# First local attention of a hybrid network: values as narrow weights on four column strips, probabilities weighed by GpSimd, output head-major in one bank

## The chip, the cores and the metric

The kernel runs on one core of one Trainium2 chip. The time is device time in microseconds of one execution, from the start of the program to its end. A core has TensorE (matmuls; its clock is granted at one of two levels, 1.2 or 2.4 GHz, and the profile shows the share), VectorE, ScalarE and GpSimd (elementwise work), and SyncE, which issues DMAs. In the profile they are PE (with its weight loads as PEld), DVE, ACT, POOL and SP. They run unsynchronised, each through its own program in order, and wait for each other on semaphores. TensorE writes to PSUM, eight banks of 128 partitions by 512 fp32; GpSimd doesn't read PSUM in this kernel.

## What is computed

A network of eight blocks in a row on x of 4 sequences ("lanes") by 512 tokens by 128 features, each block a layer norm, a sub-network and a residual. The change touches the first sub-network alone: four layers of attention and MLP. Of its 8 heads, each 16 wide, four are local (a window of 128 tokens looks at itself and at the window before it, causally), four are causal linear attention over buckets of 64 tokens:

```python
def local_attn(q, k, v):                       # heads 0 to 3, WINDOW 128
    bq, bk, bv = ...                           # windows of 128 tokens
    bk2, bv2 = look_around(bk), look_around(bv)  # window before, own window
    dots = jnp.einsum('bwie,bwje->bwij', bq, bk2) * e ** (-0.5)
    dots = jnp.where(causal_mask | pad_mask, mask_value, dots)
    attn = jax.nn.softmax(dots, axis=-1)
    return jnp.einsum('bwij,bwje->bwie', attn, bv2)

def causal_linear_attn(q, k, v):               # heads 4 to 7, BUCKET 64
    q, k = softmax(q), elu(k) + 1.0
    ctx = cumsum(einsum('bhund,bhune->bhude', bk, bv)) / (cumsum(k) + 1e-06)
    ctx = ...                                  # moved on by one bucket, zeros first
    return einsum('bhund,bhude->bhune', bq, ctx)

def self_attention(x, Wq, Wk, Wv, Wo, bo):
    out = jnp.concatenate([lo, go], axis=1)    # the eight heads' outputs
    return out @ Wo + bo
```

The blocks behind it are a mixture of experts (twice), two attentions with relative positions, a windowed attention with an MLP (twice), and a Hyena-like block of convolutions by DFT.

## The kernel before, in words

Everything lies in SBUF with features on the partitions: `inner[:, lane, token]` is the residual stream of the first stage. A planner, `make_plan`, writes one list of steps; each engine walks through it and executes the steps for which it has a function. So the order of `add(...)` in `stage_a` is the program order on every engine. PSUM tiles are numbered in that order too; the planner gives each tile the bank whose newest tile is oldest, and `take(k)` on TensorE waits for the semaphore with which the last reader of that bank's earlier tile reports (`LAST_READ`). A reader waits for `tile_full` in `full(k)`.

In a layer, `i` runs over 16 windows, four (`w`) of each lane (`c`), and three steps more. In step `i` TensorE does, in this order: the scores of window `i` (four matmuls, one per head, one bank each), the turn of window `i-1` (eight transposes of the probabilities in two banks; four in a lane's first window, which has no window before it), the values of window `i-2`. After these comes, at `w` 0, `norm_scale` of the lane two before; at `w` 1, `a_context` (transposes of q and 16 matmuls for the linear heads' context); at `w` 2, `a_project` of the next lane (q, k and the token-major qkv, four banks) and `a_out` of the lane before; at `w` 3, `norm_mean` of the lane before. The other engines have the same order: VectorE masks the scores and finds their maximum (L1516, into SA), ScalarE takes the exponential with its sum (L1247, SA to PA), both engines copy one half of the turned probabilities each to TA (ScalarE L1217, VectorE L1524).

`a_values` holds, per head and block, the turned probabilities as weights (128 by 128) and the values (128 by 16) as the moving operand, then two matmuls of 64 by 64 for the linear heads. VectorE inverts the sums, scales the local part and copies the rest to ON, token-major (L1532, L1533, L1536). `a_out` transposes the four windows of ON (L863), ScalarE copies the turned tile to AT, and only then the output projection follows (`wt(s, WA, "o")` times AT), whose result VectorE adds to `inner` (L1447). An fp32 matmul shows as two MATMUL records in the trace, a transpose as one.

GpSimd has nothing here but the norm's gain and bias (L1788). SyncE's queue holds no transfer of a window. The block of relative attention further on (its values are 128*32 matmuls over four groups of output partitions) and the windowed attention (its probabilities are multiplied by GpSimd, L1869) are not changed.

## Time and profile before

| | us |
|---|---|
| median of 3 runs | 3130.52 (3129.12 to 3149.68) |
| the profiled execution | 3123.45, of which its span is 3121.7 |
| first stage's layers, in the trace | 26 to 663 of the span |
| TensorE busy in the span | 2882.0 (92%) |
| VectorE, ScalarE, GpSimd busy | 1969.7, 1873.3, 965.9 |

The trace's views are read like this. A timeline row has the start, the length and the number of merged instructions, and in brackets how long the engine sat idle ahead of it and for whom. TensorE's records overlap and their ends are modelled, so what a piece of its work takes is the start of the next row less its own start. A group's row has its busy time (overlaps counted once), the mean length of one instruction, and the idle time ahead of the group by what ended it. A windows row has the busy time of each engine in a stretch, with the number of instructions, then the granted clock.

### The profile page before, as it was taken

How to read it: one execution, taken by the hardware profiler on the slowest of the kernel's cores; microseconds unless marked ns; L12 is line 12 of the kernel's file. 1: busy time of each engine (PE TensorE's matmuls, PEld its weight loads, DVE VectorE, ACT ScalarE, POOL GpSimd, SP SyncE). 2: the span in 40 equal slices, each digit the busy share in tenths (PEclk: the TensorE clock that was granted, in tenths of full speed). 3: DMA queues.
4: the chain of work that ended last, by engine and by line, in shares of the span. 5: the costliest groups of instructions: out<-in, count | busy, mean ns of one | idle time of the engine just before them, and what ended most of it. 6: DMA issues, size and time to landing. Idle time of an engine off the chain costs nothing.

```text
span 3121.7 us, 58985 instructions
## 1 busy us (share of the span) xinstructions
PE 2882.0 (92%) x21844; PEld 2000.2 (64%) x21844; DVE 1969.7 (63%) x5736; ACT 1873.3 (60%) x4388; POOL 965.9 (31%) x812
## 2 busy tenths in 40 slices
PE   8999999987999999879999999899899898998997
PEld 5767675743888888548888888555445464554554
DVE  5445454536677777568878787677377424764774
ACT  5464646541466666227767777577577533875774
POOL 1010101010232332025555555255255212552551
PEclk9999999988799999889999999999999999998999
DMA  1010000000000000100000000221021001210210
GB/s 51 1 39 1 12 1 9 1 4 8 1 2 2 2 2 2 50 22 2 2 2 2 2 2 2 90 54 42 13 60 45 1 22 45 51 36 13 57 41 14
DMA packets 35263, 62.85 MB, mean 20 GB/s; under 512 B 11526, under 2 KB 15654, under 8 KB 33830
## 3 DMA queue, kind: packets, MB, share of 16 engines
q1 hardware_dynamic: 34982, 59.07, 6.9%
q8 instruction: 180, 2.95, 0.4%
q14 instruction: 101, 0.83, 0.1%
HBM read 23.48 MB, written 1.15 MB: 8 GB/s over the span
## 4 chain that ended last, share of the span: by engine, by line
PE 78%; DVE 7%; ACT 6%; issue 3%; POOL 3%; SPq 2%; DMA 1%; DVEq 0%; POOLq 0%; ACTq 0%
PE bank L766 67%; PE bank L984 5%; PE bank L1099 3%; SPq L732 2%; POOL work L1869 2%; PE bank L836 1%; ACT work L1217 1%; DVE work L1583 1%; ACT bank L1225 1%; ACT squared L1227 1%; ACT work L1338 1%; DVE work L1727 1%; ACT squared L1324 0%; DVE low L1640 0%; DVE normed L1465 0%
## 5 line engine op out<-in xcount | busy, mean ns | idle before, releaser
L766 PEld LDWEIGHTS bank<-work 128*64 128x64 f32 (+3 forms) x4992 | 418.3, 163 | 186.0 <-issue 140.2
L766 PE MATMUL bank<-work 128*64 128x128 f32 (+8 forms) x4992 | 518.9, 291 | 18.4 <-ACT work L1217 8.7
L1302 ACT ACTIVATE low<-bank,low 128x512 f32<-128x512 f32 (+23 forms) x384 | 227.4, 592 | 339.2 <-DVE low L1640 335.5
L1217 ACT ACTIVATE low<-bank 128x512 f32<-128x512 f32 (+3 forms) x512 | 425.4, 941 | 1.7 <-PE bank L984 1.7
L766 PE MATMUL bank<-table_keys,halves 128*128 128x512 f32 (+3 forms) x1536 | 422.1, 384 | 0.8 <-ACT low L1302 0.8
L1640 DVE TENSOR_REDUCE low<-bank 128x1 f32<-128x512 f32 (+22 forms) x512 | 288.8, 572 | 167.2 <-PE bank L766 161.8
L1217 ACT ACTIVATE work<-bank 128x512 f32<-128x512 f32 (+5 forms) x469 | 246.8, 546 | 155.2 <-PE bank L766 59.6
L1830 POOL TENSOR_TENSOR halves<-squared,const 128x512 fp32r<-128x512 f32 x128 | 135.5, 1059 | 570.6 <-PE bank L766 570.5
L1788 POOL TENSOR_SCALAR normed<-normed,slot 128x512 f32<-128x512 f32 x48 | 75.4, 1571 | 703.4 <-DVE normed L1465 703.1
L766 PEld LDWEIGHTS bank<-table_keys,halves 128*128 128x128 f32 x1536 | 248.8, 194 | 56.8 <-issue 33.8
L1338 ACT ACTIVATE work<-work 128x192 f32<-128x192 f32 (+1 forms) x512 | 218.8, 431 | 46.7 <-DVE work L1720 46.7
L1869 POOL TENSOR_TENSOR work<-work 128x768 f32<-128x768 f32 x128 | 187.7, 1466 | 188.7 <-DVE work L1731 185.7
L766 PE MATMUL bank<-work,slot 128*128 128x512 f32 x408 | 199.3, 624 | 35.3 <-ACT work L1217 29.1
L1618 DVE TENSOR_SCALAR low<-low 128x512 f32<-128x512 f32 (+23 forms) x384 | 206.8, 539 | 13.5
L1221 ACT ACTIVATE squared<-centered 128x512 f32<-128x512 f32 x80 | 50.1, 630 | 270.2 <-DVE centered L1458 269.9
L766 PE MATMUL bank<-halves 128*128 128x128 f32 (+27 forms) x1024 | 207.3, 284 | 3.1 <-DVE halves L1633 3.1
L766 PEld LDWEIGHTS bank<-halves 128*128 128x128 f32 x1024 | 185.6, 193 | 37.2 <-DVE halves L1633 10.3
L766 PE MATMUL bank<-normed,slot 128*128 128x512 f32 x440 | 205.7, 611 | 1.7 <-POOL normed L1788 1.7
L1874 POOL TENSOR_TENSOR work<-work 128x512 f32<-128x512 f32 x128 | 169.6, 1325 | 96.1 <-DMA work<-work 84.1
L766 PE MATMUL bank<-low,table_low 128*64 128x128 f32 x1792 | 188.0, 286 | 0.5 <-DVE slot L1625 0.5
L1247 ACT ACTIVATE work<-work 128x256 f32<-128x256 f32 (+1 forms) x256 | 119.9, 469 | 108.8 <-DVE work L1516 108.8
L984 PE MATMUL bank<-const,low 128*128 128x128 f32 x1248 | 181.0, 275 | 3.1 <-ACT low L1217 3.1
(195 smaller groups left out, 5630.9 us busy)
## 6 DMA issues: line engine op xcount, KB each, us to landing
work<-work SPq DMA_DIRECT2D x512, 64.0 KB, 2.0
slot<-in_wW SPq DMA_DIRECT2D x4, 1605.5 KB, 6.8
slot<-in_wA SPq DMA_DIRECT2D x4, 837.0 KB, 6.1
table_low<-embv_padded SPq DMA_DIRECT2D x2, 1536.0 KB, 6.3
table<-in_dft SPq DMA_DIRECT2D x1, 3072.0 KB, 12.6
slot<-in_wE SPq DMA_DIRECT2D x2, 584.0 KB, 3.7
const<-in_const SPq DMA_DIRECT2D x1, 1094.0 KB, 5.3
squared<-in_x SPq DMA_DIRECT2D x4, 256.0 KB, 6.3
```

Of the source, the lines that this page charges most:

```text
L766: return pe.matmul(o, l, r, start=start, stop=stop)
L984: last = pe.transpose(o[:, b * P:(b + 1) * P], PR[t.G % 4][:, b * P:(b + 1) * P], ident)
L1099: last = pe.transpose(o[:, (2 * a + blk) * P:(2 * a + blk + 1) * P], PW[:, s.n % 3, 2 * u + a, blk * P:(blk + 1) * P], ident)
L1217: return act.activation(dst, src, ACT.Identity)
L1247: last = act.activation(PA[:, i, h, lo:256], SA[:, i, h, lo:256], ACT.Exp, scale=-1.0, bias=small_a[:, s.i % 4, h:h + 1], accum_out=small_ ...
L1302: act.activation(PR[t.G % 4][:, 0:n], bank[t.G % 2][:, 0:n], ACT.Exp, bias=NBR[:, t.G % 4:t.G % 4 + 1], accum_out=RSR[:, t.G % 8:t.G % 8 + ...
L1338: last = act.activation(row, row, ACT.Exp, scale=-1.0, bias=small[:, one:one + 1], accum_out=small[:, 4 + one:5 + one])
L1618: dve.tensor_scalar(row, row, inverse, None, ALU.mult).then_inc(sem("r_normal"), 1)
L1640: dve.tensor_reduce(out=NBR[:, t.G % 4:t.G % 4 + 1], in_=bank[t.G % 2][:, 0:score_columns(t)], axis=AX.X, op=ALU.max, negate=True).then_in ...
L1830: pool.tensor_tensor(A4[:, half, Q % 2, :].rearrange("p (t h) -> p t h", h=HEADS_R), bc(one_lane.unsqueeze(2), [P, 4 * QG, HEADS_R]), bc(k ...
L1869: pool.tensor_tensor(row, row, bc(small_w[:, s.n % 4, 8:12].unsqueeze(2), [P, 4, 192]), ALU.mult).then_inc(sem("w_weighed"), 1)
L1874: pool.tensor_tensor(R1[:, s.n % 3, :], R1[:, s.n % 3, :], R2[:, s.n % 3, :], ALU.add).then_inc(sem("w_added"), 1)
```

## The change

1. Scores of two heads share a bank: two PSUM tiles a window instead of four. VectorE writes the masked scores straight to PA, which now has three buffers; ScalarE's exponential works in place there.
2. A new step `a_weigh`: VectorE inverts the four sums right after the exponentials of the same window, and GpSimd multiplies the window's probabilities in PA by them, in place (128 by 1024 elements; 512 in a lane's first window). The turn waits for that (`a_weighed`) instead of for the exponential.
3. The turn moves from behind the scores to the end of its step.
4. Values: the values (128 by 16) are the weights, the turned probabilities the moving operand, and head `h` writes partitions 32h to 32h+16, all windows of a lane side by side in one bank, held from the first window to the last. The linear heads' context CN is laid out so that one matmul per bucket (64 by 128 weights, 64 columns moving) fills all partitions; it comes ahead of the local heads' matmuls and opens the accumulation. These tiles live in banks 6 and 7, everything else of a window in banks 0 to 5.
5. VectorE's scaling and copy to ON, the four transposes of `a_out` (L863) and its second tile are gone. A new step `a_heads`, right behind a lane's last values, is ScalarE's copy of the held bank to AT; `a_out` is the projection alone, its weight rows permuted on the host.
6. CN's zeros are written once, not once per lane.

```diff
@@ -124,10 +124,10 @@
...
-    "a_scores": each("a_scored", LOC),
+    "a_scores": (("a_scored", LOC, 2), ("a_scored", LOC, 4)),
...
-    "a_values": (("a_normalised", 1, 1),),
-    "a_out": (("a_heads", 1, 1),) + STREAM,
+    "a_values": (("a_heads", 1, 1),),
+    "a_out": STREAM,
...
         for name, a, b in LAST_READ.get(kind, ()):
-            b_ = min(HELD if kind == "w_values" else state["pool"], key=lambda one: (newest[one], one))
+            b_ = min(HELD if kind in ("a_values", "w_values") else state["pool"], key=lambda one: (newest[one], one))
...
@@ -210,6 +210,8 @@
         norm(**first)
         for layer in range(DEPTH_A):
             load = state["load"]
+            state["pool"] = SHORT
+            held = None
...
-                if 1 <= i <= C * NT:
-                    add("a_turn", c=(i - 1) // NT, w=(i - 1) % NT, i=i - 1)
                 if 2 <= i <= C * NT + 1:
-                    add("a_values", c=(i - 2) // NT, w=(i - 2) % NT, i=i - 2)
+                    if (i - 2) % NT == 0:
+                        held = add("a_values", c=(i - 2) // NT, w=0, i=i - 2)
+                    else:
+                        add("a_values_on", c=(i - 2) // NT, w=(i - 2) % NT, i=i - 2, tile=held)
+                    if (i - 2) % NT == NT - 1:
+                        add("a_heads", c=(i - 2) // NT, tile=held)
...
+                if i < C * NT:
+                    add("a_weigh", c=c, w=w, i=i)
+                if 1 <= i <= C * NT:
+                    add("a_turn", c=(i - 1) // NT, w=(i - 1) % NT, i=i - 1)
+            state["pool"] = range(BANKS)
...
-        CN = carve(NB_A, 64)
-        SA, PA = carve(2, LOC, 256), carve(2, LOC, 256)
+        PA = carve(3, LOC, 256)
         TA = carve(2, 2, T)
-        ON = carve(2, NT, P)
...
+        CN = carve(NB_A, LOC, 2, DH_A)
...
                 for h in range(LOC):
-                    mm(take(s.k + h)[:, lo:256], QL[:, b, h, s.w * P:(s.w + 1) * P],
-                       KL[:, b, (s.w - 1) * P + lo:(s.w + 1) * P]).then_inc(tile_full, 1)
+                    if h % 2 == 0:
+                        o = take(s.k + h // 2)
+                    last = mm(o[:, 256 * (h % 2) + lo:256 * (h % 2) + 256], QL[:, b, h, s.w * P:(s.w + 1) * P],
+                              KL[:, b, (s.w - 1) * P + lo:(s.w + 1) * P])
+                    if h % 2:
+                        last.then_inc(tile_full, 1)
...
             def a_turn(s):
-                i = s.i % 2
-                pe.wait_ge(sem("a_exp"), s.n + 1)
+                i = s.i % 3
+                pe.wait_ge(sem("a_weighed"), s.n + 1)
...
+            def window_values(s, o, n):
+
+                i, b = s.i % 2, s.c % 2
+                lane = n // NT
+                pe.wait_ge(sem("a_context_done"), lane + 1)
+                pe.wait_ge(sem("a_q_turned"), lane + 1)
+                for u in (2 * s.w, 2 * s.w + 1):
+                    mm(o[:, u * BUCKET:(u + 1) * BUCKET], CN[0:64, u].rearrange("p h a d -> p (h a d)"),
+                       QT[0:64, u * BUCKET:(u + 1) * BUCKET], start=(u == 2 * s.w), stop=False)
+                pe.wait_ge(sem("a_turned_act"), n + 1)
+                pe.wait_ge(sem("a_turned_dve"), n + 1)
+                for blk in range(0 if s.w else 1, 2):
+                    for h in range(LOC):
+                        last = mm(o[32 * h:32 * h + DH_A, s.w * P:(s.w + 1) * P],
+                                  TM[:, b, s.w - 1 + blk, P + h * DH_A:P + (h + 1) * DH_A],
+                                  TA[:, i, h // 2, (2 * (h % 2) + blk) * P:(2 * (h % 2) + blk + 1) * P],
+                                  start=False, stop=(blk == 1))
+                return last
+
             def a_values(s):
-                i, b = s.i % 2, s.c % 2
-                pe.wait_ge(sem("a_turned_act"), s.n + 1)
-                pe.wait_ge(sem("a_turned_dve"), s.n + 1)
-                o = take(s.k)
-                for h in range(LOC):
-                    for blk in range(0 if s.w else 1, 2):
-                        mm(o[:, h * DH_A:(h + 1) * DH_A],
-                           TA[:, i, h // 2, (2 * (h % 2) + blk) * P:(2 * (h % 2) + blk + 1) * P],
-                           TM[:, b, s.w - 1 + blk, P + h * DH_A:P + (h + 1) * DH_A],
-                           start=(blk == (0 if s.w else 1)), stop=(blk == 1))
-                pe.wait_ge(sem("a_context_done"), s.n // NT + 1)
-                pe.wait_ge(sem("a_q_turned"), s.n // NT + 1)
-                for e in range(2):
-                    u = 2 * s.w + e
-                    last = mm(o[64 * e:64 * e + 64, 64:128], QT[0:64, u * 64:(u + 1) * 64], CN[0:64, u, :])
-                last.then_inc(tile_full, 1)
+                window_values(s, take(s.k), NT * s.n).then_inc(tile_full, 1)
+
+            def a_values_on(s):
+                window_values(s, tile_of(s.tile.k), NT * (s.n // (NT - 1)) + s.w).then_inc(sem("a_valued"), 1)
 
             def a_out(s):
-                b = s.c % 2
-                pe.wait_ge(sem("a_normalised"), NT * (s.n + 1))
-                o = take(s.k)
-                for w in range(NT):
-                    last = pe.transpose(o[:, w * P:(w + 1) * P], ON[:, b, w, :], ident)
-                last.then_inc(tile_full, 1)
                 pe.wait_ge(sem("a_heads"), s.n + 1)
-                mm(take(s.k + 1)[:, :], wt(s, WA, "o"), AT).then_inc(tile_full, 1)
+                mm(take(s.k)[:, :], wt(s, WA, "o"), AT).then_inc(tile_full, 1)
...
-            def a_out(s):
-                copy(AT, full(s.k)[:, :]).then_inc(sem("a_heads"), 1)
+            def a_heads(s):
+                act.wait_ge(sem("a_valued"), (NT - 1) * (s.n + 1))
+                copy(AT, tile_of(s.tile.k)[:, :]).then_inc(sem("a_heads"), 1)
...
@@ -1501,19 +1515,23 @@
 
             def a_context(s):
                 o = full(s.k + 1)[0:64, 0:455].rearrange("p (u f) -> p u f", u=NB_A - 1)
-                dve.memset(CN[0:64, 0, :], 0.0)
+                if s.n == 0:
+                    link(dve.memset(CN[0:64], 0.0))
+                own = CN[0:64, 1:8, :, 1, :]
                 link(dve.tensor_scalar(kcum[0:64, 0:7], o[:, :, 64], 1e-6, None, ALU.add))
                 dve.reciprocal(kcum[0:64, 0:7], kcum[0:64, 0:7])
-                dve.tensor_tensor(CN[0:64, 1:8, :], o[:, :, 0:64], bc(k_("linear_mask")[0:64].unsqueeze(1), [64, 7, 64]),
+                heads = "p u (h d) -> p u h d"
+                dve.tensor_tensor(own, o[:, :, 0:64].rearrange(heads, h=LOC),
+                                  bc(k_("linear_mask")[0:64].rearrange("p (h d) -> p h d", h=LOC).unsqueeze(1), [64, 7, LOC, DH_A]),
                                   ALU.mult).then_inc(sem("a_context_read"), 1)
                 dve.wait_ge(sem("a_context_read"), s.n + 1)
-                dve.tensor_tensor(CN[0:64, 1:8, :], CN[0:64, 1:8, :], bc(kcum[0:64, 0:7].unsqueeze(2), [64, 7, 64]),
+                dve.tensor_tensor(own, own, bc(kcum[0:64, 0:7].unsqueeze(2).unsqueeze(3), [64, 7, LOC, DH_A]),
                                   ALU.mult).then_inc(sem("a_context_done"), 1)
...
-                    dve.tensor_tensor_reduce(out=SA[:, i, h, lo:256], in0=full(s.k + h)[:, lo:256],
+                    dve.tensor_tensor_reduce(out=PA[:, i, h, lo:256], in0=full(s.k + h // 2)[:, 256 * (h % 2) + lo:256 * (h % 2) + 256],
...
-            def a_values(s):
-                b = s.c % 2
-                o = full(s.k)
-                inverse = small_a[:, 8 + s.i % 2, 0:LOC]
-                link(dve.reciprocal(inverse, small_a[:, 4 + s.i % 4, 0:LOC]))
-                dve.tensor_tensor(ON[:, b, s.w, 0:64].rearrange("p (h d) -> p h d", h=LOC),
-                                  o[:, 0:64].rearrange("p (h d) -> p h d", h=LOC),
-                                  bc(inverse.unsqueeze(2), [P, LOC, DH_A]), ALU.mult)
-                dve.tensor_copy(ON[:, b, s.w, 64:128], o[:, 64:128]).then_inc(sem("a_normalised"), 1)
+            def a_weigh(s):
+                dve.wait_ge(sem("a_exp"), s.n + 1)
+                dve.reciprocal(small_a[:, 8 + s.i % 4, 0:LOC], small_a[:, 4 + s.i % 4, 0:LOC]).then_inc(sem("a_inverted"), 1)
...
+            def a_weigh(s):
+                lo = 0 if s.w else P
+                pool.wait_ge(sem("a_inverted"), s.n + 1)
+                row = PA[:, s.i % 3, :, lo:256]
+                pool.tensor_tensor(row, row, bc(small_a[:, 8 + s.i % 4, 0:LOC].unsqueeze(2), [P, LOC, 256 - lo]), ALU.mult)\
+                    .then_inc(sem("a_weighed"), 1)
...
-            "o": A["Wo"][i], "w1": A["W1"][i], "w2": rows(A["W2"][i]), "bo": column(A["bo"][i]),
```

How it stands in the programs. TensorE at `w` 2 of lane 1 in the first layer: values of the lane's first window, the projections of lane 2, the output of lane 0. L766 and L774 are the same helper, `mm`; L836 and L848 the turn; the names in brackets are semaphores. Before:

```order
L766 MATMUL bank<-work 128x16 [waits a_q_turned,a_turned_dve,a_turned_act]
L766 MATMUL bank<-work 128x16 x3
L766 MATMUL bank<-work 64x64 [waits a_q_turned,a_context_done]
L766 MATMUL bank<-work 64x64
L766 MATMUL bank<-normed,slot 128x512 [waits a_context_read,norm_done]
...
L766 MATMUL bank<-slot,normed 128x256
L863 MATMUL bank<-const,work 128x128 [waits a_scored,a_normalised]
L863 MATMUL bank<-const,work 128x128 x3
L766 MATMUL bank<-work,slot 128x512 [waits a_turned_act,a_heads]
```

After:

```order
L774 MATMUL bank<-work 128x64 [waits a_q_turned,a_context_done,norm_centered]
L774 MATMUL bank<-work 128x64
L774 MATMUL bank<-work 16x128 [waits a_turned_dve,a_turned_act]
L774 MATMUL bank<-work 16x128 x3
L774 MATMUL bank<-normed,slot 128x512 [waits a_q_turned,norm_done]
...
L774 MATMUL bank<-slot,normed 128x256
L774 MATMUL bank<-work,slot 128x512 [waits a_scored,a_heads]
L848 MATMUL bank<-const,work 128x128 [waits a_scored,a_weighed]
L848 MATMUL bank<-const,work 128x128 x3
```

The context now goes first and with 64 columns, the values are 16 output rows wide; the four transposes and the copy between them and the projection are gone, and the turn of window 1, which stood ahead of the values, now ends the step and waits for GpSimd.

VectorE at `w` 3 of lane 1, from the last instruction of `a_linear` (L1499, now L1513) on. L1524 and L1542 are the copy of the turned half, L1458 and L1472 the norm's centering. Before:

```order
L1499 SCALAR_TENSOR_TENSOR work<-work 128x256
L1524 COPY work<-bank 128x512
L1532 RECIPROCAL work<-work 128x4
L1533 TENSOR_TENSOR work<-bank,work 128x64
L1536 COPY work<-bank 128x64
L1458 TENSOR_TENSOR centered<-inner,bank 128x512
```

After:

```order
L1513 SCALAR_TENSOR_TENSOR work<-work 128x256
L1472 TENSOR_TENSOR centered<-inner,bank 128x512
L1548 RECIPROCAL work<-work 128x4
L1542 COPY work<-bank 128x512
L1534 ISA work<-bank,const 128x128
```

The copy of the turned half, which stood right behind `a_linear`, now stands behind the centering and behind the reciprocal of the newest window; the scaling and the copy to ON are gone. GpSimd's program gets 64 new instructions of this stage, one per window, between its 32 of the norms.

## Rows read from the trace of the kernel before

**Rows 1.** The page: busy time of the engines, and the chain that ended last.
```profile
PE 2882.0 (92%) x21844; PEld 2000.2 (64%) x21844; DVE 1969.7 (63%) x5736; ACT 1873.3 (60%) x4388; POOL 965.9 (31%) x812
...
PE 78%; DVE 7%; ACT 6%; issue 3%; POOL 3%; SPq 2%; DMA 1%; DVEq 0%; POOLq 0%; ACTq 0%
```

**Rows 2.** Two stretches by windows, a layer's windows and its MLP: us, PE, PEld, DVE, ACT, POOL busy, clock.
```profile
190.00:301.00 111.00, 103.99 (x723) 85.86 (x723) 64.52 (x254) 61.40 (x184) 6.25 (x4) 0.97 0.00 1
301.00:352.00 51.00, 46.52 (x119) 21.30 (x118) 11.70 (x22) 29.92 (x40) 6.25 (x4) 0.90 0.05 17
```

**Rows 3.** TensorE in order of time, windows of the second layer (columns: start, us).
```profile
249.03 1.89 PE L766 MATMUL bank<-work 128*128 128x256 f32 x8
250.76 0.60 PE L836 MATMUL bank<-const,work 128*128 128x128 f32 x4
251.20 2.12 PE L766 MATMUL bank<-work 128*128 128x16 f32 x20
253.25 0.63 PE L808 MATMUL bank<-const,work 128*64 128x128 f32 x4
253.80 4.84 PE L766 MATMUL bank<-work 64*64 64x65 f32 x40
258.48 1.04 PE L836 MATMUL bank<-const,work 128*128 128x128 f32 x8
259.36 1.22 PE L766 MATMUL bank<-work 128*128 128x16 f32 x12
260.51 1.98 PE L766 MATMUL bank<-normed,slot 128*128 128x512 f32 x4
...
264.06 0.60 PE L863 MATMUL bank<-const,work 128*128 128x128 f32 x4
267.27 1.13 PE L766 MATMUL bank<-work,slot 128*128 128x512 f32 x2 [2.61 <-ACT work L1217]
268.23 1.46 PE L766 MATMUL bank<-work 128*128 128x256 f32 x6
```

**Rows 4.** TensorE's groups by shape, first stage: the group that waits for ScalarE.
```profile
L766 PE MATMUL bank<-work,slot 128*128 128x512 f32 x160 | 82.9, 651 | 32.6 <-ACT work L1217 26.4 <-ACT work L1265 6.1
```

**Rows 5.** TensorE in order of time, relative attention: two strips, then four.
```profile
910.30 0.66 PE L766 MATMUL bank<-low,table_low 128*64 128x128 f32 x8
910.89 1.08 PE L766 MATMUL bank<-low 128*32 128x128 f32 x32
911.78 0.63 PE L766 MATMUL bank<-slot,const 128*32 128x64 f32 x32
```

**Rows 6.** TensorE after a wait in lane 1, and the granted clock there.
```profile
236.20 2.07 PE L766 MATMUL bank<-work,slot 128*128 128x512 f32 x2 [2.61 <-ACT work L1217]
238.07 2.47 PE L766 MATMUL bank<-work 128*128 128x256 f32 x8
240.37 0.82 PE L836 MATMUL bank<-const,work 128*128 128x128 f32 x6
```

**Rows 7.** That stretch in the windows view; the granted clock is third from the end.
```profile
236.00:240.00 4.00, 3.80 (x9) 2.47 (x10) 1.47 (x4) 0.52 (x2) 0.00 (x0) 0.60 0.00 0
```

**Rows 8.** VectorE's groups by shape, first stage: count, busy, mean ns.
```profile
L1516 DVE CUSTOM_DVE_ANT_0 work<-bank,const 128x256 f32<-128x256 f32 x192 | 71.5, 417 | 0.7
L1524 DVE COPY work<-bank 128x512 f32<-128x512 f32 x48 | 32.9, 685 | 3.4 <-PE bank L836 3.1
...
L1447 DVE SCALAR_TENSOR_TENSOR inner<-bank,slot,inner 128x512 f32<-128x512 f32 x32 | 24.0, 751 | 147.0 <-PE bank L766 147.0
```

**Rows 9.** ScalarE's groups by shape, first stage.
```profile
L1247 ACT ACTIVATE work<-work 128x256 f32<-128x256 f32 x192 | 95.1, 496 | 103.6 <-DVE work L1516 103.6
...
L1221 ACT ACTIVATE squared<-centered 128x512 f32<-128x512 f32 x32 | 20.0, 630 | 85.1 <-DVE centered L1458 85.1
```

**Rows 10.** The page: the costliest groups, of the window attention further on.
```profile
L1869 POOL TENSOR_TENSOR work<-work 128x768 f32<-128x768 f32 x128 | 187.7, 1466 | 188.7 <-DVE work L1731 185.7
```

**Rows 11.** TensorE's groups by shape, whole span: the turn of the window attention.
```profile
L1099 PE MATMUL bank<-const,work 128*128 128x128 f32 x896 | 125.6, 282 | 46.8 <-POOL work L1869 46.8
```

18 lines of the change are left out of this document (9 added, 9 removed).

## The prediction

> **What bounds the kernel now.** I read the page first, then the windows view of the first stage, then TensorE's order of time inside it. On the page TensorE is busy for 92% of the span and holds 78% of the chain that ended last [rows 1]. In a layer's windows it is busy for 104 of 111 us while VectorE has 65, ScalarE 61 and GpSimd 6; in the MLP behind them 47 of 51, at a granted clock of 0.90 [rows 2]. The order of time shows how it is filled [rows 3]: from 249.03 to 264.06 each row starts where the work ahead of it has streamed out, 1.73 us for a window's scores, 0.88 for its turn (0.44 in a lane's first window), 2.05 for its values (251.20 to 253.25; 1.15 in a first window), 3.55 for the projections. TensorE waits for nobody there. The one hole is in `a_out`: 3.21 us from 264.06 to 267.27, of which the transposes are 0.44. So in this stage whatever shortens TensorE's own work or closes that hole is worth its full length, and whatever the other three engines gain or lose counts only once it makes TensorE wait.
>
> **The change part by part, one layer being 16 windows, four layers 64.**
>
> *Values.* Rows 3 give two equations: 20 records in 2.05 us, 12 in 1.15, so a record of the 128x16 kind costs 0.11 us. It streams 16 columns only; it is the 128 columns of weights that take the time. The other four (the linear heads) cost 0.25 with the change of the array's shape. Now the weights are 16 wide and 128 columns stream. The nearest row is the relative attention's: 32 records of 128*32 with 128 columns from 910.89 to 911.78, 0.028 us each [rows 5]. Four of them run at a time, since one alone, at the 0.11 us that a 128-column transpose takes (0.88 for eight, rows 3), could not be faster than 0.11. The order there is the one here, four strips in turn. So 16 records cost 0.45 us, and eight 0.22. The linear heads now load 128 columns: between 0.25 as before and 4 x 0.11 = 0.45 for records bound by such loads; I take 0.45, as the shape is that of the loads that bind today. There is one more change of the array's shape per window (128 rows, 64 rows, 128 rows in strips, 128 rows: three, not two). From 910.30 to 910.89 eight records on two strips take 0.59 us where half the four-strip pace allows 0.44 [rows 5], so a change costs 0.15; I add 0.25 for the one more and the longer way out, between 0.15 and 0.35. A full window is then 0.45 + 0.45 + 0.25 = 1.15 instead of 2.05, a first one 0.92 instead of 1.15: 48 x 0.90 + 16 x 0.23 = 47 us gained. With the dear ends it is 40, with the cheap ones 62. The Trainium skill, "TensorEngine Tiling (Array Packing)", Key Properties, says that a change of tiling mode drains the array. The trace agrees, and that is the 0.15.
>
> *The output.* The four transposes and ScalarE's copy leave the space between the projections and the output. ScalarE stood in that space behind five projection copies and an exponential that waits for VectorE. The group by shape shows 26.4 us of idle time of TensorE for that copy [rows 4], which is 8 x 2.61 + 8 x 0.69: two long ones per layer (lanes 0 and 1, behind a projection, each 3.21 us with the transposes) and two short ones (lane 2; lane 3 at the layer's end, nothing to hide it), each about 1.34. The new copy is asked for a whole step earlier, at `w` 1, with the context's 3.4 us and more behind it [rows 3], and is covered. Gained: 8 x 3.21 + 4 x 1.34 = 31 us. In lane 3 the hole stays as a wait for the copy.
>
> *The clock.* Behind the long hole that ends at 236.20 the granted clock is 0.60 over 4 us [rows 7], most of it at the 1.2 GHz level, after TensorE had stood idle for 2.6 us; the pair of output matmuls takes 1.87 us where it takes 0.96 at 267.27, the scores 2.30 instead of 1.73 [rows 3, 6]. That is 1.5 us, and by the clock of the layers' windows (0.97 in rows 2) it occurs once in a layer from the second on: 4.5 us back.
>
> *Waits that may come.* The turn now wants VectorE's reciprocal and GpSimd's product. GpSimd's nearest row is the same multiplication of the window attention, 1.466 us for 768 elements [rows 10], so 1.95 for 1024 and 1.0 for 512. I walk the dearest place, the steps `w` 2 and 3 of lanes 1 and 2, from the start of `w` 2. TensorE: scores to 1.7, values to 2.7, projections to 6.2, output to 7.2, turn to 8.1. VectorE: from 6.2 a copy (0.69, as L1524) and three instructions over 256 elements (0.42, as L1516) to 8.2, residual 0.75 to 8.95, reciprocal to 9.1, turned half to 9.9 [rows 8]. GpSimd has the window's product at 11.1; TensorE wants it at 8.1 + 1.7 + 1.15 + 0.96 = 11.9, in time. Next, VectorE: four scores to 11.4, `a_linear` (four of 0.42) to 13.1, centering (0.69 too, as long as a copy) to 13.8, reciprocal and turned half to 14.7; ScalarE squares (0.63) behind the centering [rows 9], then copies its half, to 15.0. TensorE, done with `w` 3 at 12.8, has scores of 0.9 and the linear heads' 0.6 and wants both halves at 14.4: it waits 0.6 to 0.7. Queued behind VectorE's wait are its own copy of the turned half and the next scores; TensorE alone waits for them. With two such places per layer, half a microsecond in lane 0 (no `a_out` covers GpSimd there) and at the layer's start, it is 2.3 us per layer, 9 in all. Lower bound 0. Upper bound by the windowed attention, where the turn waits for GpSimd in the same way: 46.8 us in 128 steps [rows 11], 0.37 each, 23 us for 64.
>
> *At nothing.* Shared score banks and three PA buffers: the matmuls are the same ones, VectorE starts half a microsecond later and is hidden. Six banks instead of eight: walking the reuse, the last reader of each is done before TensorE asks; the nearest is the bank of the first projection, which ScalarE reads in four copies during the other projections and the turn asks for at 7.6. If that cover were gone, it would cost one such copy, 0.6 us, in three lanes per layer, 7 us. VectorE loses two instructions per window, GpSimd has 110 of 637 us more to do: neither binds. The layer's end: GpSimd's 2 us come in, transposes and VectorE's scaling go out, and the held bank makes the copy wait for the last window as before; I count it even, already at the lower clock. No DMA moves.
>
> **Sum.** 47 + 31 + 4.5 - 9 = 73.5 us off the profiled execution's 3123.5 gives 3050. The timed runs had their median 7.0 above it, at 3130.5. So 3057 for the median.
>
> **The rivals.**
>
> *The turn waits at every window* (0.12). The chain from the last exponential over VectorE's reciprocal, GpSimd and the turn to the copies is longer by 2 us and two handovers. For it: VectorE stands in that chain behind a residual or a norm. Against it: a step of TensorE is 5.8 us on average, and my walk has it 0.8 in hand. At 0.7 us per window it costs 45 instead of 9: 3093.
>
> *Slower than before* (0.04). One mechanism: GpSimd's product lands late in every window. It must cost TensorE more than (73.5 + 9) / 64 = 1.3 us per window to eat all. The walk has 0.8 in hand, so that needs a product of over 4.05 us instead of 1.95, a pace that no row shows. At 4.5 us it is 1.75 per window on 3048 (the forecast without waits): 3160.
>
> *Strips of 16 don't overlap* (0.04). Then 16 records cost 16 x 0.11 = 1.76 us, a window's values 2.46 instead of 2.05, and the 47 gained become 48 x 0.41 + 16 x 0.43 = 27 lost: 3130.5 + 27 - 31 - 4.5 + 9 = 3131. That is the case that the change does nothing. Rows 5 speak against it, with strips of 32 columns full. The Trainium skill, "TensorE: Matmul & The Clock Gate", Part 3, states that a weight load overlaps matmuls in flight only when the row group differs; here all strips have the same rows, so by that rule this rival would hold. The row disagrees with it: 0.028 us per record, loads included.
>
> *The lower clock at the layer's end goes as well* (0.08). Its MLP stretch has 0.90 over 51 us [rows 2], so 10 us at the lower level, about 5 us lost, in four layers. If the fuller windows ahead prevent it: 20 more, 3037. Against it: the waits at the layer's end, which stand directly ahead of it, remain.
>
> **How the numbers follow.** The forecast has 0.72, its own range 3040 to 3075: gain of the values 40 to 62, waits 0 to 23. The prediction is its time, 3057. The range of 3035 to 3095 takes in the clock's rival and the waiting one and leaves out under 0.2. A change of 1% (31 us) is about what a measurement of this kernel tells from none. Faster by more than that, under 3099: nearly all of the forecast, the clock's rival and most of the waiting one, 0.89. Within 1%: the strips' rival and a rest of the waiting one, 0.07. Slower: 0.04.
>
> **What would show it.** In TensorE's order of time after: a window's 16 records of 128*16 with 128 columns in about 0.45 us, the 64*128 ones in about 0.45; no L863 row, and the projection's pair following the qkv records directly; no window of 0.60 in lane 1. The idle time that the turn spends on GpSimd and the values on VectorE or ScalarE under 10 us together in the stage; a product of GpSimd of 1.95 us; the time from the stage's start to its end down from 637 to about 563. I'd be wrong if 128*16 records stand 0.1 us apart, if the turn's group has over 20 us of idle time, or if the clock falls below 0.97 in the windows, which were full before and need TensorE's work for it.

## The result, and the profile after

| | before | after |
|---|---|---|
| median of the timed runs, us | 3138.0 (3129.12 to 3149.68, 4 runs) | 3046.38 (3043.49 to 3047.78, 4 runs) |
| the profiled execution, and its span | 3123.45, 3121.7 | 3047.78, 3046.0 |
| first stage, from 25 us to the start of its last residual | to 662.5 | to 582.8 |

The changed kernel takes 0.9705 of the time, 95% interval 0.9664 to 0.9745. The kernel before was timed once more beside it, which brought its median from 3130.5 to 3138.0. The forecast was 3057, range 3035 to 3095. The stage ends 79.7 us earlier in the profiled pair, and what follows it takes 4 us longer. The page of the changed kernel, the answer to [rows 1]:

```profile
PE 2821.3 (93%) x21780; PEld 1916.9 (63%) x21780; DVE 1939.3 (64%) x5593; ACT 1875.2 (62%) x4388; POOL 1072.7 (35%) x876
```

TensorE lost 61 us of busy time, GpSimd gained 107 and still has two thirds of the span free. The windows view of the whole first stage (columns as in [rows 2]; the clock is third from the end):

```profile
25.00:583.00 558.00, 525.85 (x3285) 340.06 (x3283) 272.94 (x961) 363.75 (x893) 164.71 (x97) 0.98 0.03 9
```

The same view of the kernel before:

```profile
25.00:662.00 637.00, 589.12 (x3347) 421.79 (x3345) 303.52 (x1103) 362.40 (x891) 57.10 (x33) 0.96 0.03 8
```

So TensorE's busy time fell by 63 us and its idle time by 16. TensorE in order of time in lanes 0 and 1 of the second layer, the answer to [rows 3]:

```profile
231.82 1.02 PE L774 MATMUL bank<-normed,slot 128*128 128x512 f32 x2
232.68 1.89 PE L774 MATMUL bank<-slot,normed 128*128 128x256 f32 x8
234.41 1.02 PE L774 MATMUL bank<-work,slot 128*128 128x512 f32 x2
235.27 1.04 PE L848 MATMUL bank<-const,work 128*128 128x128 f32 x8
...
244.04 1.04 PE L848 MATMUL bank<-const,work 128*128 128x128 f32 x8
244.91 3.04 PE L774 MATMUL bank<-work 128*128 128x256 f32 x28
247.88 0.63 PE L816 MATMUL bank<-const,work 128*64 128x128 f32 x4
...
251.79 2.82 PE L774 MATMUL bank<-work 128*128 128x256 f32 x20
254.54 0.70 PE L774 MATMUL bank<-work,slot 128*128 128x512 f32 x1
```

The output pair (234.41) follows the qkv records with no hole and no transposes. The row of 244.91 merges eight records of scores, four of 64\*128 and 16 of 128\*16. It is 2.97 us to the next row. Less the scores' 1.73 [rows 3], a full window's values take 1.24 us, where they took 2.05. In a lane's first window (251.79, eight records of 128\*16) it is 2.75 less 1.73, so 1.02 instead of 1.15. The values' group of the kernel before, and its four transposes ahead of each output:

```profile
L766 PE MATMUL bank<-work 128*128 128x16 f32 x896 | 104.5, 257 | 0.0
L863 PE MATMUL bank<-const,work 128*128 128x128 f32 x64 | 11.9, 317 | 2.8 <-DVE work L1536 2.8
```

TensorE's groups by shape over the stage (25 to 583 us), the answer to [rows 4]:

```profile
L774 PE MATMUL bank<-work,slot 128*128 128x512 f32 x160 | 77.2, 613 | 9.4 <-ACT work L1279 6.4 <-ACT work L1230 2.8
L848 PE MATMUL bank<-const,work 128*128 128x128 f32 x448 | 60.6, 275 | 2.0 <-POOL work L1882 2.0
L774 PE MATMUL bank<-work 64*128 64x64 f32 x256 | 41.9, 284 | 0.5 <-issue 0.5
L774 PE MATMUL bank<-work 128*16 128x128 f32 x896 | 36.9, 275 | 7.8 <-DVE work L1542 5.6 <-ACT work L1230 2.2
```

The wait for the output's copy went from 26.4 us to 2.8, what is left being the copy at the layer's end. The turn waits 2.0 us for GpSimd in the whole stage. New is 5.6 for VectorE's copy of the turned half, L1542. It is one wait per layer, at its end (columns: start, length):

```profile
265.51 0.75 DVE L1479 SCALAR_TENSOR_TENSOR normed<-centered,slot,squared 128x512 f32<-128x512 f32 x1 [3.44 <-ACT squared L1240]
266.18 0.68 DVE L1542 COPY work<-bank 128x512 f32<-128x512 f32 x1
267.01 0.63 PE L774 MATMUL bank<-work 128*16 128x128 f32 x16 [1.40 <-DVE work L1542]
268.35 1.94 PE L774 MATMUL bank<-work,slot 128*128 128x512 f32 x2 [0.71 <-ACT work L1230]
```

VectorE's norm scale of lane 2 (L1479) waits 3.44 us for ScalarE's part of that norm, and the copy that the last values want stands behind it. GpSimd's product, by its groups in the same stretch:

```profile
L1882 POOL TENSOR_TENSOR work<-work 128x1024 f32<-128x1024 f32 x48 | 90.9, 1894 | 169.0 <-DVE work L1548 168.7
L1882 POOL TENSOR_TENSOR work<-work 128x512 f32<-128x512 f32 x16 | 16.6, 1041 | 6.9 <-DVE work L1548 5.9
```

### The profile page after: what moved, and what is told of

Read it like the earlier page. It is cut to its first block, busy times and chain, and to the rows that moved or that the text cites. A ratio compares the mean times of both kernels' runs of the same rounds, so it can differ in the third digit from the quotient of the medians.

```text
span 3046.0 us, 58762 instructions
## 1 busy us (share of the span) xinstructions
PE 2821.3 (93%) x21780; PEld 1916.9 (63%) x21780; DVE 1939.3 (64%) x5593; ACT 1875.2 (62%) x4388; POOL 1072.7 (35%) x876
## 3 DMA queue, kind: packets, MB, share of 16 engines
HBM read 23.48 MB, written 1.15 MB: 8 GB/s over the span
## 4 chain that ended last, share of the span: by engine, by line
PE 77%; DVE 8%; ACT 5%; POOL 3%; issue 3%; SPq 2%; DMA 1%; DVEq 0%; POOLq 0%; ACTq 0%
PE bank L774 66%; PE bank L997 6%; PE bank L1112 3%; SPq L740 2%; POOL work L1888 2%; PE bank L848 1%; ACT work L1230 1%; DVE work L1595 1%; ACT bank L1238 1%; ACT squared L1240 1%; DVE work L1739 1%; ACT work L1352 1%; DMA work<-work 1%; DVE centered L1472 1%; ACT squared L1234 0%
## 5 line engine op out<-in xcount | busy, mean ns | idle before, releaser
L774 PE MATMUL bank<-work 128*64 128x128 f32 (+8 forms) x4992 | 468.9, 297 | 26.5 <-ACT work L1230 10.7
L774 PEld LDWEIGHTS bank<-work 128*64 128x64 f32 (+4 forms) x4992 | 350.3, 149 | 195.6 <-issue 147.2
L774 PE MATMUL bank<-table_keys,halves 128*128 128x512 f32 (+3 forms) x1536 | 420.7, 383 | 1.0 <-ACT low L1316 1.0
L774 PEld LDWEIGHTS bank<-table_keys,halves 128*128 128x128 f32 x1536 | 247.3, 193 | 56.6 <-issue 33.3
L774 PE MATMUL bank<-halves 128*128 128x128 f32 (+27 forms) x1024 | 206.6, 284 | 3.1 <-DVE halves L1645 3.1
L774 PEld LDWEIGHTS bank<-halves 128*128 128x128 f32 x1024 | 184.7, 192 | 37.4 <-DVE halves L1645 10.5
L774 PE MATMUL bank<-work,slot 128*128 128x512 f32 x408 | 196.6, 617 | 12.1 <-ACT work L1279 6.4
L774 PE MATMUL bank<-normed,slot 128*128 128x512 f32 x440 | 202.2, 602 | 1.7 <-POOL normed L1800 1.7
L774 PE MATMUL bank<-low,table_low 128*64 128x128 f32 x1792 | 187.1, 286 | 0.5 <-DVE slot L1637 0.5
L1112 PEld LDWEIGHTS bank<-const,work 128*128 128x128 f32 x896 | 107.5, 146 | 108.9 <-POOL work L1888 64.9
```

What stands on the lines that cost most here:

```text
L774: return pe.matmul(o, l, r, start=start, stop=stop)
L1112: last = pe.transpose(o[:, (2 * a + blk) * P:(2 * a + blk + 1) * P], PW[:, s.n % 3, 2 * u + a, blk * P:(blk + 1) * P], ident)
```

## The experiments

A "strip" below is one group of 32 output partitions, of which a head's values fill 16. Where the values' gain comes from, whether the hole was worth what it showed, whether the product is hidden and how near it is to the bound, and what the clock does, were put to runs. The time at 1.2 GHz below is summed from the granted clock between 25 us and the start of the stage's last residual, in the one profiled execution of each kernel; so is the stage's end. All ratios are to the kernel before as it was timed in the same batch.

| kernel | median us | ratio, 95% | stage ends | at 1.2 GHz |
|---|---|---|---|---|
| before (first profile / again) | 3138.0 / 3136.8 | 1 / 0.9998 | 662.5 / 671.6 | 54.6 / 71.7 |
| after (first profile / again) | 3046.4 / 3045.3 | 0.9705 / 0.9696 [0.9680, 0.9712] | 582.8 / 583.1 | 17.1 / 20.5 |
| one strip | 3113.3 | 0.9911 [0.9894, 0.9928] | 645.8 | 3.4 |
| output late, on before | 3107.8 | 0.9887 [0.9860, 0.9914] | 651.4 | 81.9 |
| no product | 3046.8 | 0.9698 [0.9678, 0.9719] | 582.9 | 27.3 |
| product twice | 3089.1 | 0.9830 [0.9804, 0.9855] | 619.9 | 13.7 |
| both ends | 3039.1 | 0.9673 [0.9657, 0.9689] | 580.1 | 17.1 |
| heads outer | 3053.5 | 0.9715 [0.9698, 0.9732] | 586.7 | 27.3 |
| turn early | 3261.7 | 1.0392 [1.0368, 1.0415] | 812.1 | 286.7 |
| hole filled, on before | 3138.7 | 0.9997 [0.9982, 1.0012] | 672.1 | 75.1 |
| end filled | 3037.0 | 0.9671 [0.9652, 0.9691] | 574.8 | 6.8 |
| tail order | 3038.9 | 0.9683 [0.9663, 0.9704] | 573.2 | 3.4 |

**Do the strips run at the same time?** All heads write to the first strip, so that every matmul follows another on the same columns (the flags that open and close the accumulation change with it). The four heads' outputs are then summed on one strip.

```diff
-                        last = mm(o[32 * h:32 * h + DH_A, s.w * P:(s.w + 1) * P],
+                        last = mm(o[0:DH_A, s.w * P:(s.w + 1) * P],
```

> The changed kernel, but all four local heads write the same 16 output partitions, so that all their matmuls stand on one column strip (the output is then not the reference's: the heads' values are added together). Same matmuls, same shapes, same order. Theory (the values' gain is four strips running at once): the 16 records of a full window stand 0.107 us apart, as one 128-column stream does, so the group takes 1.8 us instead of the 0.56 seen after the change, a first window's eight 0.95 instead of 0.34: 48 x 1.25 + 16 x 0.6 = 70 us more, about 3116 us. Rival (narrow weights are what is cheap, not the strips): the records stay under 0.05 us apart and the time stays within 10 us of 3046.

Measured 3113.3, 67 us above the changed kernel, the records of a window now 0.110 us apart. The group by shape over its stage (25 to 646 us), the same 896 records:

```profile
L774 PE MATMUL bank<-work 128*16 128x128 f32 x896 | 108.9, 273 | 7.8 <-DVE work L1542 5.6 <-ACT work L1230 2.1
```

108.9 us of busy time against 36.9. So the gain of the values comes from the four strips' overlap. With the roles swapped and one strip, a record costs about what it cost before (0.106 us apart there).

**Was the hole worth its length?** In the kernel before, the output projection alone is moved behind the next window's scores and turn, so that ScalarE's copy has their time.

```diff
+                if w == 3 and 1 <= c:
+                    add("a_out", c=c - 1, tile=held)
                 if 2 <= i <= C * NT + 1:
                     add("a_values", c=(i - 2) // NT, w=(i - 2) % NT, i=i - 2)
@@
                 if w == 2 and 1 <= c:
-                    add("a_out", c=c - 1)
+                    held = add("a_out_turn", c=c - 1)
```

> The kernel before, with one thing changed: the output projection of a lane stands behind the next window's scores and turn, not directly behind its transposes, so that ScalarE's copy has 2.6 us of TensorE's work to hide behind (the last lane of a layer has it directly behind as before). Theory (the hole is worth its length, since TensorE waits for nothing else): 8 x 2.77 + 4 x 0.85 = 25.6 us, and 4.5 us for the lower clock behind three of the holes: 30 us less than before, ratio 0.990. Rival (the hole moves: scores or norms wait instead): under 12 us less.

Measured 3107.8, 34 us below the 3142 of the kernel before in the same batch. The group that waited 32.6 us in [rows 4], here over 25 to 651 us:

```profile
L771 PE MATMUL bank<-work,slot 128*128 128x512 f32 x160 | 79.7, 630 | 9.0 <-ACT work L1272 6.0 <-ACT work L1224 2.7
```

23.7 us of the 26.4 are gone with the transposes left in, near the 25.6 expected; the rest of the 34 is not explained by these waits. The execution profiled was the slowest of the four (3119.3 us). Its time at the lower clock is no shorter than before (81.9 us): the holes went and the clock did not rise, so the 4.5 us expected from the clock are not seen.

**Is the product hidden?** GpSimd's program without it; the turn waits for the exponential. The local heads' outputs are then not normalised.

```diff
-                pe.wait_ge(sem("a_weighed"), s.n + 1)
+                pe.wait_ge(sem("a_exp"), s.n + 1)
```

> The changed kernel without GpSimd's product (so the probabilities are not divided by their sum, and the output is not the reference's); the turn waits for the exponentials directly, VectorE's reciprocal stays. Theory (the product is hidden but for two windows at each layer's start, where the turn starts 0.06 us behind it and TensorE shows gaps of 0.32 and 0.38 us): 3 to 5 us less, 3042 us. Rival (the turn waits at every window): 20 us less or more.

Measured 3046.8, the changed kernel's own time. 107 us of new work on GpSimd cost nothing that can be measured. The 3 to 5 us expected could not have been told from nothing: the interval of the ratio is 6 us wide to either side. In the profile the turn's 2.0 us of waiting are gone.

**How near is it to the bound?** The product is made twice, one behind the other, so that the probabilities are divided twice.

```diff
+                    .then_inc(sem("a_weighed_once"), 1)
+                pool.wait_ge(sem("a_weighed_once"), s.n + 1)
+                pool.tensor_tensor(row, row, bc(small_a[:, 8 + s.i % 4, 0:LOC].unsqueeze(2), [P, LOC, 256 - lo]), ALU.mult)\
```

> The changed kernel with GpSimd's product of each window done twice in a row, 1.9 us more in the chain of a full window, 1.05 in a first one (the output is not the reference's). Theory: in the trace of the changed kernel the turn starts 0.06 to 5.5 us behind the product's end; what a window lacks of 1.95 (1.1) us is 51.6 us summed over the 64 windows, so 40 to 52 us more, about 3093. If the product were covered with much to spare, under 10 us more; if the turn waited at every window already, 64 windows would cost 108 us more, 3154.

Measured 3089.1, 43 us more. The turn's group over its stage:

```profile
L848 PE MATMUL bank<-const,work 128*128 128x128 f32 x448 | 62.9, 281 | 38.9 <-POOL work L1885 38.9
```

An extra 1.9 us per window cost 0.6 of wait on average. In the changed kernel's second layer the product ends 2.2 to 5.5 us ahead of the turn in the first two windows of lanes 1 and 2, 0.85 to 0.94 us in the other two, 0.5 to 2.2 in lane 3, and 0.06 in the last two of lane 0.

**Does the place of the turn matter?** The turn back to where it stood, directly behind the next window's scores, and gone from the end of the step.

```diff
                 if i < C * NT:
                     add("a_scores", c=c, w=w, i=i)
+                if 1 <= i <= C * NT:
+                    add("a_turn", c=(i - 1) // NT, w=(i - 1) % NT, i=i - 1)
```

> The changed kernel with the turn put back directly behind the scores of the next window; all else stays. If the prediction's reason for the later place of the turn holds, the turn now waits for GpSimd's weighing: from the end of the last exponential the weighing still takes 1.9 us for a 128x1024 tile, and TensorE has only the scores (0.5 us) ahead of the turn where it had scores and values (1.8 us). About 1.3 us in most of the 64 windows: 60 to 80 us more than the changed kernel, 3105 to 3125 us, ratio to the kernel before 0.990 to 0.995, with GpSimd's product as the releaser of the turn's idle time. Rival: the weighing is finished early enough in any place, since lanes 1 to 3 showed 0.5 to 5.5 us of slack: within 15 us of the changed kernel, 3046 to 3060.

Measured 3261.7: slower than before, and 216 us above the changed kernel where 60 to 80 were expected. TensorE's turn over the stage, by shape:

```profile
L848 PE MATMUL bank<-const,work 128*128 128x128 f32 x448 | 77.2, 324 | 112.4 <-POOL work L1882 112.4
```

One window in order of time:

```profile
253.39 1.89 PE L774 MATMUL bank<-work 128*128 128x256 f32 x8
257.52 1.10 PE L848 MATMUL bank<-const,work 128*128 128x128 f32 x8 [2.23 <-POOL work L1882]
```

And the windows view of the stage:

```profile
25.00:812.00 787.00, 653.57 (x3283) 413.15 (x3281) 280.08 (x960) 370.88 (x891) 164.54 (x97) 0.82 0.02 6
```

The theory holds and the rival does not: 56 of the 64 turns start 0.05 us behind the end of GpSimd's product. The size was wrong twice. These turns wait 2.0 us each and not 1.3, which is 110 us more than in the changed kernel. And the clock fell to 0.82 for the stage: the same instructions keep TensorE busy for 653.6 us instead of 525.9, 128 more, with 286.7 us at 1.2 GHz instead of 17. So in this run a wait in nearly every window went with a loss of its length and as much again.

**Were the first profiles typical?** Both kernels were run again, unchanged.

> The kernel before, unchanged, for a second profile: its profiled execution took 3123.5 us, but its timed runs beside the experiments have their median at 3142. Theory (TensorE's clock differs from execution to execution): the new profile is longer, with more time at the lower granted clock than the first (a span clock under 0.963), and TensorE's gaps in the first stage, such as 2.88 us behind the transposes, are the same to 0.01 us. Rival (something else, such as slower transfers or engines): the same clock share, and longer gaps or longer instructions.

> The changed kernel, unchanged, as the yardstick for the next one on the same chip. Theory: 3046 us within 3 us, a ratio of 0.970 to the kernel before; its second profile has the same gaps in the first stage (0.81, 1.67 and 0.98 us at each layer's end), and only the stretches at the lower clock may lie elsewhere.

The kernel before: 3136.8, stage to 671.6 and not 662.5. Its holes have the same length (2.61 us idle each), but 71.7 us of the stage lie at 1.2 GHz, 17.1 more. The stage is 9.1 us longer. The changed kernel repeats itself (583.1, 20.5 us). So the gain in the stage is 80 us in the first pair and 88 in the second. The rest of the program differs by 4 and 5 us, to either side.

**Is the lower clock the holes' doing?** In the kernel before, two matmuls without use fill the hole of lanes 0 and 1, on the output's own bank.

```diff
+                if s.c < 2:
+                    for _ in range(2):
+                        mm(o[:, :], ident, const[:, 0:T])
```

> The kernel before with two matmuls without use (identity by 512 columns, into the output's own bank, which the projection overwrites) in the 2.8 us hole ahead of the output projections of lanes 0 and 1; their time lies inside the hole, so that the chain waits as long as before. If the 2.8 us holes cost a second time through the clock, the stretches at 1.2 GHz behind these eight holes go, and with them 1 to 1.5 us each: 8 to 12 us less than the kernel before, ratio 0.996 to 0.9975. Rival: the clock falls for another reason (the long holes at the layers' ends), or what is in the hole does not matter: ratio 1.000, and the stretches stay.

Measured 3138.7, ratio 0.9997: no gain where 8 to 12 us were expected, and the rival's time holds. TensorE in order of time:

```profile
233.34 1.88 PE L766 MATMUL bank<-const 128*128 128x512 f32 x4
236.12 1.12 PE L766 MATMUL bank<-work,slot 128*128 128x512 f32 x2 [0.89 <-ACT work L1221]
```

Three stretches of that kernel by windows:

```profile
236.00:240.00 4.00, 3.88 (x22) 3.15 (x22) 2.68 (x11) 1.66 (x8) 0.00 (x0) 1.00 0.00 0
...
252.70:259.50 6.80, 6.80 (x37) 5.54 (x36) 2.21 (x9) 1.03 (x4) 0.00 (x0) 0.50 0.00 0
303.90:317.60 13.70, 11.41 (x30) 6.12 (x30) 2.72 (x6) 4.03 (x6) 1.56 (x1) 0.50 0.00 0
```

The hole shrank to 0.89 us of idle time, the fall right behind it is gone (1.00 where [rows 7] had 0.60), and the clock fell at 252.7 instead, for 6.8 us and not 3.4, in full work. In the three later layers the fall at the layer's end is longer too, 13.7 us where it was 10.2. The sum, 75.1 us, is that of the kernel before again (71.7). Together with "output late" (no hole, 81.9) this says that the holes behind the projections are not what most of the lower clock hangs on.

Where it lies, the clock's own stretches show. In both profiles of the kernel before, the clock is at 1.2 GHz for 10.2 us at the end of each of the four layers, 41.0 us of the 54.6 and of the 71.7. In the changed kernel it is so for 6.8 us at the end of two layers, 13.7 in all. One such end before, and one after:

```profile
304.10:314.30 10.20, 8.07 (x12) 3.40 (x13) 1.95 (x6) 2.54 (x4) 1.56 (x1) 0.50 0.01 2
268.50:275.30 6.80, 5.96 (x7) 2.06 (x8) 1.44 (x2) 1.25 (x2) 0.00 (x0) 0.50 0.00 0
```

By the change, the layer's end lost the transposes with their wait for VectorE (2.8 us in four layers), and the values' matmuls in it and ahead of it are others. Every profile with the old values has the old layer's end too, so no run says which of the two brought the 41.0 down.

**Does the order of the strips matter?** The head's loop outside, the block's inside, so that each strip gets two matmuls, four records, in a row.

```diff
-                for blk in range(0 if s.w else 1, 2):
-                    for h in range(LOC):
+                for h in range(LOC):
+                    for blk in range(0 if s.w else 1, 2):
```

> The changed kernel with the two loops of the local heads' matmuls exchanged: head outside, block inside. In a full window four records in a row then go to one strip, where now two do; a lane's first window is unchanged. Theory A (matmuls start in program order, so strips overlap only where neighbours in the program are on different ones): a full window's 16 records take at least 13 x 0.107 = 1.4 us instead of 0.56, 48 x 0.83 = 40 us more, 3086. Theory B (the order among the strips does not matter): no change, 3046.

Measured 3053.5, stage to 586.7. The group by shape (25 to 587 us):

```profile
L774 PE MATMUL bank<-work 128*16 128x128 f32 x896 | 37.9, 275 | 7.8 <-DVE work L1542 5.6 <-ACT work L1230 2.2
```

One microsecond more in 896 records, 25 ns apart where they were 24: the pace hardly depends on the order. The other 3 us in the stage go with 7 to 10 us more at 1.2 GHz; whether the order causes these can't be told from one profile.

**Can the layer's end be mended?** First, both ends: the norm scale of lane 2 goes behind the last turn, and at a layer's start the previous norm's steps go ahead of the first scores.

```diff
-                if w == 0 and 2 <= c:
+                if w == 0 and 2 <= c < C:
                     add("norm_scale", c=c - 2, **second)
@@
+                if w == 0 and c == C:
+                    add("norm_scale", c=c - 2, **second)
```

> The changed kernel with two steps moved. At a layer's end the norm_scale of lane 2 stands behind the last turn, so VectorE copies the last turned half without waiting for that norm's root (TensorE's wait before the last values is 1.67 - 0.11 = 1.5 us in every layer). At the start of the second to fourth layer the norm_scale of lane 2 and the norm_mean of lane 3 stand ahead of the first scores, in the 2.2 us in which TensorE waits for ScalarE's copies. Theory (TensorE's holes are worth their length): 4 x 1.4 + 3 x 1.8 = 11 us less than the changed kernel, 3035. Rival (the moved steps hold up something else, or the waits shift): within 3 us of it.

Measured 3039.1, 6 us below the changed kernel and not 11. At the start the wait was only moved: of the 6.8 us for ScalarE's copies 5.1 went, and 6.7 came behind the first scores, for VectorE's linear heads. So the edit shown was run alone ("tail order"), and with one matmul without use in each of two remaining holes of the layer's end ("end filled", here that of the output):

```diff
+                if s.c == C - 1:
+                    mm(o[:, :], ident, const[:, 0:T])
```

> The changed kernel with VectorE's order at the layer's end alone changed (the norm's scale of lane 2 behind the copy of the last turn). In the run with the edits at both ends that hole went from 1.67 to 0.55 us, and a new wait of 2.5 us stood at the layer's start. Without the edit at the start: 4 x 1.1 = 4.5 us less than the changed kernel, about 3041 us, ratio 0.968. Rival: the second norm of lane 2 comes later and the wait goes there: 3045 us.

> The changed kernel with two edits: at a layer's end VectorE makes the norm's scale of lane 2 behind the copy of the last turn (so that lane 3's last values don't wait 1.67 us for that copy), and TensorE gets two matmuls without use ahead of lane 3's output projection and ahead of the mean of lane 3's second norm. The order alone is worth 4 x 1.1 = 4 to 5 us; if the clock behind the layer's end stays at its high level thanks to the filling, 3 to 5 us more: 3036 to 3038 us, ratio 0.967. Rival: the filling delays the chain by its own 0.4 us in each place and the clock does as before: 3041 to 3045.

Tail order: 3038.9. Its groups by shape over the stage:

```profile
L850 PE MATMUL bank<-const,work 128*128 128x128 f32 x448 | 60.8, 276 | 3.1 <-POOL work L1884 3.1
L776 PE MATMUL bank<-work 128*16 128x128 f32 x896 | 36.9, 275 | 2.2 <-ACT work L1232 2.2
```

The 5.6 us for VectorE's copy are gone, 1.1 stands at GpSimd's product instead: 4.5, as expected. The stage ends at 573.2, 10 us earlier, with 3.4 us at 1.2 GHz instead of 17 to 20. At a layer's end the clock does not fall in this profile, nor in those of "both ends" and "end filled"; it did in two layers of each profile of the changed kernel, which has the wait of 1.40 us there, and in four of "no product". "One strip" has that wait and no such fall, so the wait alone does not decide it. End filled: 3037.0, stage to 574.8, 6.8 us at 1.2 GHz. The filling can't be told from the order alone. Both medians lie 6 to 9 us under the changed kernel's, and the intervals of the ratios overlap with that of the changed kernel, so the gain is clearer in the stage than in the whole.

## Why the prediction was right

**What bounds the stage.** Right. TensorE alone counted: 107 us more on GpSimd moved nothing that can be measured ("no product": 3046.8). That the instructions less on VectorE gained nothing by themselves was not put to a run.

**The values, 47 us.** Right in mechanism, 6 too high. 48 x 0.81 + 16 x 0.13 = 41. The 128\*16 group has 36.9 us for 64 windows, 0.58 on average, near what was taken with its share of the change. The 64\*128 group has 41.9, so 0.65 busy per window with the overlap of its neighbours; from the first of its records to the first 128\*16 one it is 0.58 us where 0.45 was put. From the first 64\*128 record to the end of the values a full window takes 1.15 us, as forecast; what was left out is 0.09 in the scores ahead, which take 1.82 us where they took 1.73 before, now that the array's shape changes behind them. The first window's 0.92 was 1.02. The row of the relative attention [rows 5] was the right one for strips of 16: "one strip" put the rival to the test and gave 67 us more than the changed kernel, where the rival had 74 more than the forecast. The cheap end of this term, 62, is missummed: by its own terms a full window is 0.85 and a first one 0.62, which gives 66. The Trainium skill, "TensorE: Matmul & The Clock Gate", Part 3, says that a weight load overlaps matmuls in flight only when the row group differs. Here it is the same for all strips, and the trace disagrees: 36.9 us on four strips against 108.9 on one, loads included.

**The output, 31 us.** Right. The wait for the copy fell by 23.6 us, and the 64 transposes' 64 x 0.11 = 7 went. With them went 2.8 us that TensorE waited for VectorE's copy to ON at the layers' ends, which the prediction had counted even. "Output late" gave that hole's part alone.

**The clock, 4.5 us.** The term that was mis-sized, and its reason does not hold. The three stretches that it counted are in the trace of the kernel before, 3.4 us each at 1.2 GHz at 235.8, 396.2 and 556.7, and gone after. What it left out of the sum is the layer's end, 41.0 us at 1.2 GHz before and 13.7 after. In all, the time at 1.2 GHz in the stage fell from 54.6 to 17.1 us in the profiled pair, from 71.7 to 20.5 in the second. The busy time fell by 63 us, of which 41 are the values and 7 the transposes, so about 15 are the clock. By the two executions of the kernel before, 9.1 us for 17.1, it would be 20. The reason given was the hole in front of the stretch: "hole filled" and "output late" showed such stretches move while the sum stays. What did bring it down is open.

**Waits, 9 us.** The size was right, the places wrong. The new idle time is 7.8 + 2.0 + 0.5 = 10.3 us. Of the 0.6 to 0.7 us twice per layer in lanes 1 and 2 nothing came: the rows from 235.27 to 254.54 have no bracket. VectorE and ScalarE were a little faster than in the walk: the later half of the turned probabilities is there 14.2 us after the start of step `w` 2, where the walk had 15.0, and TensorE wants it at 14.4. The 0.8 us that the walk had in hand for GpSimd's product are 0.85 to 0.94 in the trace. In lane 0 the turn waits for the product, 2.0 us in all, as was said. The other 7.8 are the layer's end, counted even. There the walk did not follow VectorE through the norm scale that stands ahead of the copy, once per layer 1.40 us for VectorE's copy and 0.54 for ScalarE's.

**The sum.** 41 + 31 + 3 + 15 - 10 = 80 beside the 79.7 of the stage and the 75.7 of the profiled spans, where 73.5 were forecast. The 15 is what is left of the busy time, so only the idle side is a check: 23.6 + 2.8 - 10.3 = 16.1 beside 15.7. That 73.5 came so near is in part luck: 6 too much for the values stood against 10 too little for the clock and 3 for the transposes' wait. The profiled execution after took 3047.8 where 3050 was the forecast, 2.2 less. The rest of the miss of 10.6 us is the 7.0 that were added from the profiled execution to the median: after the change the median lies 1.4 below the profiled one. The 7.0 was no constant: with a fourth run the median of before was 14.5 above the profiled execution. That one had a mean granted clock of 0.963, the timed ones of the batch with "one strip" 0.955 to 0.959, so by these figures it was a lucky execution of a kernel whose time at 1.2 GHz varies. The changed kernel varies less here (3041.7 to 3049.4 in five runs, beside 3127.1 to 3153.1 in eight). The gain of the medians, 92 to 97 us over the batches, is more than 75.7, by this reading for the same reason. The forecast's own range has a slip as well: its ends, gain of the values 40 to 66 and waits 0 to 23, give 3029 to 3078 and not 3040 to 3075.

**The rivals.** The turn that waits at every window didn't come, and "turn early" shows how near it was: the product is 1.89 us as forecast (1.95), and it is hidden only because scores, values and all else of a step stand ahead of the turn. The point from which the change loses was put at 1.3 us per window; at 1.8 us per window on average it lost, by 4%. At 1.75 that rival had put 3160 where 3262 was measured; the 128 us of TensorE's time at the lower clock were not in its price. "The lower clock at the layer's end goes as well", with a chance of 0.08, came in part and in the changed kernel itself: 41.0 us became 13.7, about two thirds of what that rival wanted. "Tail order" has none left there, and its stage ends 10 us earlier.

## What to carry to other kernels

Where a matmul streams few columns behind a full load of weights, swap the roles so that the narrow operand is loaded, and put the heads on column strips: with them four run in the time of one, without them the swap gained nothing here (3113 us, beside 3108 for the late output alone). What then needs a factor per row of the old output has to get it before the transpose, and the step that waits for it goes to the end of the loop's body; check that place by moving it, not by the idle engine's load. And take a profiled execution's distance from the median as something to explain before adding it to a forecast.

## What the runs showed of the hardware

- Matmuls of 16 output columns on four strips overlap as those of 32 do. In a full window their records stand 24 ns apart in the changed kernel and 110 ns on one strip, and the order among the strips hardly matters (36.9 and 37.9 us for 896).
- The granted clock of one program varies between executions with all waits equal: 54.6 and 71.7 us of the stage at 1.2 GHz, 9.1 us of time.
- Filling a wait of 2.6 us with matmuls moved the fall of the clock by some 17 us and didn't shorten the time at the lower level (75.1 us). With waits of 2 us in nearly every window, on the other hand, it was 286.7 us, which cost 128 us of TensorE's time on top of the 110 waited.
- GpSimd's product of 128x1024 took 1894 ns and of 128x512 1041, where its 768 elements of [rows 10] took 1466: each 256 elements more cost 0.43 us.
